# A graph-attention block with feed-forward and two normalisations: feed-forward chunks of 512 tokens in place of 256

## What is computed

```python
h = elu(gat_heads(x, adj, W_heads, a_heads))        # 4 heads, 512 features each
out = elu(gat_heads(concat(h), adj, W_out[None], a_out[None]))   # [128, 64, 512]
ffn = maximum(out @ w1 + b1, 0.0) @ w2 + b2         # 512 -> 512 -> 512
y = ffn + out
z = (y - mean(y)) / sqrt(var(y) + 1e-5) * gamma + beta
x = layernorm(x + z)                                # the output
```

## Time and profile before

| | |
|---|---|
| median of 3 runs | 2152.59 us |
| the profiled execution | 2151.31 us, span of its instructions 2149.5 us |
| TensorE busy | 2104.7 us (98% of the span) |
| VectorE, ScalarE, GpSimd busy | 1629.1 (76%), 988.9 (46%), 969.3 us (45%) |
| chain of work that ended last | TensorE 93%, VectorE 2%, GpSimd 2% |
| first feed-forward matmul | 1744.66 us from the start of the span |

### The profile page before, as it was taken

One profiled execution on the slowest core, in us unless ns is written; L12 is line 12 of the kernel. 1 busy time (PEld: TensorE's weight loads), 2 busy tenths in 40 slices (PEclk: granted clock), 3 DMA queues, 4 the chain that ended last, 5 costly groups with the idle time before them and its releaser, 6 DMA issues.

```text
span 2149.5 us, 42374 instructions
## 1 busy us (share of the span) xinstructions
PE 2104.7 (98%) x13668; PEld 1902.8 (89%) x13668; DVE 1629.1 (76%) x3297; ACT 988.9 (46%) x2282; POOL 969.3 (45%) x1017
## 2 busy tenths in 40 slices
PE   4999999999999999999999999999999999999997
PEld 2899999999999999999999999999999989999996
DVE  3877777777777777777777777777777679999998
ACT  3544444444444444444444444444444444444343
POOL 4433333333333333333333333333333347777776
PEclk7999999999999999999999999999999999999999
DMA  8111111111111111111111111111111124333342
GB/s 290 31 40 40 40 39 39 39 39 39 39 39 39 39 39 39 39 42 41 39 39 39 39 39 39 39 39 40 41 41 40 64 89 140 119 134 129 127 137 89
DMA packets 73862, 134.05 MB, mean 62 GB/s; under 512 B 8672, under 2 KB 8800, under 8 KB 73824
## 3 DMA queue, kind: packets, MB, share of 16 engines
q1 hardware_dynamic: 73824, 133.57, 18.9%
HBM read 99.98 MB, written 33.55 MB: 62 GB/s over the span
## 4 chain that ended last, share of the span: by engine, by line
PE 93%; DVE 2%; POOL 2%; issue 1%; DMA 1%; ACT 0%; SPq 0%; POOLq 0%; DVEq 0%; ACTq 0%
PE h_ps L448 11%; PE h_ps L447 11%; PE h_ps L446 11%; PE t_ps L460 11%; PE t_ps L461 11%; PE t_ps L462 11%; PE h_ps L542 3%; PE h_ps L544 3%; PE h_ps L543 3%; PE t_ps L558 2%; PE t_ps L556 2%; PE t_ps L557 2%; PE h_ps L430 1%; PE h_ps L431 1%; PE x_ps L431 1%; PE x_ps L430 1%
## 5 line engine op out<-in xcount | busy, mean ns | idle before, releaser
L1151 POOL TENSOR_TENSOR h_lo<-h_full,h_hi 128x256 fp32r<-128x256 f32 x512 | 402.8, 787 | 1012.0 <-ACT h_hi L723 998.0
L446 PE MATMUL h_ps<-g_hi,wh_hi 128*128 128x256 f32 x2048 | 585.1, 286 | 1.3 <-DVE h_full L958 0.9
L448 PE MATMUL h_ps<-g_hi,wh_lo 128*128 128x256 f32 x2048 | 578.5, 282 | 0.0
L447 PE MATMUL h_ps<-g_lo,wh_hi 128*128 128x256 f32 x2048 | 578.3, 282 | 0.0
L956 DVE TENSOR_SCALAR h_full<-h_full 128x256 f32<-128x256 f32 x512 | 247.3, 483 | 339.7 <-ACT h_full L689 338.7
L460 PE MATMUL t_ps<-wo_hi,h_hi 128*128 128x512 f32 x1024 | 404.8, 395 | 0.0
L461 PE MATMUL t_ps<-wo_lo,h_hi 128*128 128x512 f32 x1024 | 404.2, 395 | 0.0
L446 PEld LDWEIGHTS h_ps<-g_hi,wh_hi 128*128 128x128 f32 x2048 | 389.7, 190 | 16.4 <-DVE h_full L958 1.5
L447 PEld LDWEIGHTS h_ps<-g_lo,wh_hi 128*128 128x128 f32 x2048 | 390.1, 190 | 13.0
L462 PE MATMUL t_ps<-wo_hi,h_lo 128*128 128x512 f32 x1024 | 399.1, 390 | 0.0
L448 PEld LDWEIGHTS h_ps<-g_hi,wh_lo 128*128 128x128 f32 x2048 | 390.2, 191 | 0.0
(11 more groups left out here) (141 smaller groups left out, 3919.9 us busy)
## 6 DMA issues: line engine op xcount, KB each, us to landing
x_dup<-in_x SPq DMA_DIRECT2D x248, 128.0 KB, 2.5
attn<-in_x_t SPq DMA_DIRECT2D x64, 256.0 KB, 2.8
mid<-o_buf SPq DMA_DIRECT2D x64, 256.0 KB, 2.0
o_in<-mid SPq DMA_DIRECT2D x32, 512.0 KB, 3.7
x_again<-in_x SPq DMA_DIRECT2D x32, 512.0 KB, 4.3
out<-res SPq DMA_DIRECT2D x64, 256.0 KB, 2.0
wt_raw<-in_w_heads_t SPq DMA_DIRECT2D x4, 1024.0 KB, 9.3
wh_raw<-in_w_heads SPq DMA_DIRECT2D x4, 1024.0 KB, 16.4
```

The source lines that it names most:

```text
L446: mm(to, w_hi, g_hi[:, h, ft, :], start=ft == 0, stop=False)
L447: mm(to, w_hi, g_lo[:, h, ft, :], start=False, stop=False)
L448: last = mm(to, w_lo, g_hi[:, h, ft, :], start=False, stop=ft == FT - 1)
L1151: tt(h_lo[:, v % RING, :], h_full[:, v % RING, :], h_hi[:, v % RING, :].bitcast(F32), ALU.subtract)\
```

## The change

The feed-forward part goes in `FCHUNKS` = 16 chunks of `TF` = 512 tokens (`FP` = 4 pieces). The attention part is the same. In the feed-forward part:
- `hidden` uses 512 moving columns, all of a bank, and its ScalarE and GpSimd instructions are 512 wide and half as many.
- `y_ps` has four banks. The buffers of a chunk are twice as large, and some are laid over others.
- Loads are twice as large and half as many. `load_o` and `load_x_again` of chunk c + 1 now stand behind the first two stores of chunk c - 1.
- VectorE takes the norms of a chunk in two halves of two pieces. `norms(c - 1, 1)` and then `norms(c, 0)` run in the iteration of chunk c, and the four `ot_rest` of chunk c + 1 stand together between them, with the first two `y` of chunk c.
- ScalarE makes a deviation for each half: four in a chunk of 512, one of them ahead of the first hidden tile.
- Before the first chunk, four pieces are transposed in place of two, and the end of the attention part is woven into the first chunk alone.

```diff
-            hid_hi, hid_lo = sb_ff("hid_hi", [P, DT, T], F32R), sb_ff("hid_lo", [P, DT, T], F32R)
-            x_again = sb_ff("x_again", [P, 2, CP, F])
+            x_again = sb_ff("x_again", [P, 2, FP, F])
...
-        ot_ps, hid_ps, y_ps = x_ps[0], h_ps, t_ps[CHUNKS % 2]
+        ot_ps, hid_ps, y_ps = x_ps[0], h_ps, t_ps[CHUNKS % 2] + t_ps[(CHUNKS - 1) % 2]
...
             def ff_iteration(c, par, first, last):
+                if first:
+                    tail(LAST, 0)
+                    tail(LAST, 1)
+                else:
+                    save(c - 1, 0)
                 if not last and not first:
                     load_o(c + 1, 1 - par)
                     load_x_again(c + 1, 1 - par)
...
                 if not first:
-                    save(c - 1)
+                    save(c - 1, 1)
...
-                to = hid_ps[dt % 2][:, 0:T]
+                to = hid_ps[dt % 2][:, :]
...
-                zeroth, second = first_of(c), isinstance(c, int) and c == 1
-                if second:
-                    attend2(LAST, 0)
+                zeroth = first_of(c)
                 for dt in range(DT):
-                    if zeroth and dt == 3:
+                    hidden(c, dt)
+                    if zeroth and dt == 1:
                         spread2(LAST, False)
-                    if second and dt == 2:
-                        attend2(LAST, 1)
-                    hidden(c, dt)
-                for p in range(CP):
-                    if zeroth and p == 1:
-                        transpose_attn2(LAST)
+                if zeroth:
+                    transpose_attn2(LAST)
+                for p in range(FP):
                     if not last:
                         transpose_o(c + 1, 1 - par, next_turn, p)
                     result(c, p)
+                    if zeroth and p < CP:
+                        attend2(LAST, p)
...
             def ff_iteration(c, par, first, last):
-                second = isinstance(c, int) and c == 1
-                if second:
-                    out_exp(LAST, 0)
-                    t_round(LAST, LAST % 2, 1)
+                if not first:
+                    deviation(c - 1, 0, 1, mean2_done, std2_done)
                 for dt in range(DT):
...
+                    if not first and dt == 1:
+                        deviation(c - 1, 1, 0, mean_done, std_done)
...
+                    deviation(c - 1, 1, 1, mean2_done, std2_done)
+                for p in range(FP):
+                    if not last:
+                        ot_round(c + 1, p)
...
+                deviation(c, 0, 0, mean_done, std_done)
...
                 else:
-                    norms(c - 1, True, not last)
+                    sum_up(c - 1, 2)
+                    sum_up(c - 1, 3)
+                    norms(c - 1, 1)
+                for p in range(FP):
+                    if not last:
+                        ot_rest(c + 1, p)
...
+                    if p in (1, 2):
+                        sum_up(c, p - 1)
+                norms(c, 0)
```

More of the change, by code:

```diff
@@ L88, in build @@
                                            sb_ff("beta_row", [P, F]))
[L89 to L93, removed]
+            hid = sb_ff("hid", [P, 2, TF])
+            stats = sb_ff("stats", [P, 2, FP, 6])
+            moments = sb_ff("moments", [P, 2, FP, 2])
+            std = sb_ff("std", [P, 2, FP])
+            inv_std = sb_ff("inv_std", [P, 2, FP])
+            sb_ff("unused_wh", [P, 3 * F - 20 * FP])
+            o_in = sb_ff("o_in", [P, 2, FP, F])
+            hid_hi, hid_lo = sb_ff("hid_hi", [P, DT, TF], F32R), sb_ff("hid_lo", [P, DT, TF], F32R)
+            res = sb_ff("res", [P, FP, F])
         wh_lo = sb("wh_lo", [P, NH, FT, O], F32R)
@@ L115, in build @@
                 nc.sbuf_tensor("x_t_first", [P, FT, CP, P], F32R) as x_t_first:
+            pass
+        with nc.sbuf_tensor("ot_hi", [P, FT, TF], F32R) as ot_hi, \
+                nc.sbuf_tensor("ot_lo", [P, FT, TF], F32R) as ot_lo:
             pass
@@ L372, in _ @@
             load_x_again(1, 1)
[L373 to L376, removed]
+            ff_chunks(sp, ff_iteration)
+            for half in range(2):
+                save(FLAST, half)
+            for p in range(FP):
+                sp.wait_ge(store[p], 16 * FCHUNKS)
         @block.tensor
@@ L528, in transpose_o @@
                     pe.wait_ge(o_load[par], turn * 16)
-                after(pe, ot_lo_done, c * CP + p)
+                after(pe, ot_lo_done, c * FP + p)
                 for ft in range(FT):
@@ L757, in ff_iteration @@
                     if dt == 0:
-                        after(act, y_ps_done, c * CP)
+                        after(act, y_ps_done, c * FP)
                     act.activation(hid_hi[:, dt, :], hid[:, dt % 2, :], copy).then_inc(hid_hi_done, 1)
[L760 to L763, removed]
+                    if not first and dt == 1:
+                        deviation(c - 1, 1, 0, mean_done, std_done)
+                    if first and dt == 2:
+                        exps2(LAST)
                 if first:
@@ L1048, in norms, with sum_up @@
+            def sum_up(c, p):
+                dve.wait_ge(y_ps_done, c * FP + p + 1)
+                dve.wait_ge(ob_done, c * FP + p + 1)
+                tt(y[:, p, :], y_ps[p][:, :], ob[:, p, :], ALU.add).then_inc(y_done, 1)
+            def norms(c, half):
+                both = (2 * half, 2 * half + 1)
+                moments_of(c, half, 0, y, y_done, mean_done)
+                for p in both:
+                    dve.wait_ge(mean_done, c * FP + p + 1)
                     stt(z[:, p, :], y[:, p, :], moments[:, 0, p, 0:1], gamma_row[:, :], ALU.subtract,
@@ L1110, in _ @@
             dve.wait_ge(row_in, 64)
-            chunks(dve, ff_iteration)
-            norms(LAST, False, False)
+            ff_chunks(dve, ff_iteration)
+            sum_up(FLAST, 2)
+            sum_up(FLAST, 3)
+            norms(FLAST, 1)
         @block.gpsimd
```

186 lines of the change are left out of this document (89 added, 97 removed).

## The result

The changed kernel takes 2225.97 us (median of 5 runs, 2223.87 to 2229.96) against 2152.59 before: a ratio of 1.0346, 95% interval [1.0335, 1.0357]. The profiled execution took 2228.05 us, its span is 2226.3.

A forecast was written before the change was run, and what follows sets the result against it. TensorE bounds the kernel before; after, VectorE does, waiting mid-lap for TensorE. 1748.8 + 28.5 + 14 x 27.15 + 39.3 = 2196.7 us of span, plus 3.1, gives 2199.8, taken as 2200 us; range 2176 to 2233.

The forecast's parts named there:

- the ring: Loop of waits between VectorE and TensorE, one `ot_lo(0)` to the next: 27.15 us a lap, ends 25.55 to 29.35.
- A: From the end of `ot_lo(0)` to the start of `ot_lo(3)`, through TensorE's transposes and results: 7.75 us.
- E: VectorE's `norms(c, 1)`, against GpSimd's `hid_lo` and first sums: 9.3 us, between 9.16 and 9.76.
- B: VectorE's `ot_lo(3)`, from its start to the next instruction's: 0.6 us.
- D: VectorE's `y(c, 2)` and `y(c, 3)`, after the first norms: 1.2 us.
- F: VectorE's `ot_lo(0)` of the next round, closing the lap: 0.6 us.
- C: VectorE's `norms(c, 0)`, with GpSimd's sums ended before it starts: 7.7 us.
- The load: `o_in`, 1 MB, on SP's queue behind the first two stores: 5.5 us taken, hidden within 7.0 us.
- Rival 2: Load of `o_in` is the bound, from 7.0 us; at 8.5 us, 2222 us in all; chance 0.10.
- The last chunk: From TensorE's first hidden matmul of it to the last store landing: 39.3 us, nothing transposed.
- Rival 1: TensorE stays the bound, if the lap is under 23.8 us; 2148 us in all; chance 0.04.
- Rival 4: TensorE's 3.3 us of waiting per lap lowers its clock to 1.2 GHz for stretches: 2225 us; chance 0.04.

The follow-up runs named there:

- the shortest form: Changed kernel with loads ahead of stores, two banks for transposed pieces, last `ot_lo` inside `norms(c, 0)`, last `hid_lo` in two halves: 2158.43 us, 1.0034.

## Why the prediction was right, and where its sizes were off

Forecast and time lie on the same side, and the ring was there: **slower, since VectorE waits for TensorE in the middle of the lap.** By its steps:

- **A**: 7.75 us predicted, from the end of `ot_lo(0)` to the start of `ot_lo(3)`. Clean laps have 7.77 to 7.81. Six of the seven dropped laps have 9.3 to 9.4, each behind an E of 10.9: in the lap shown A is 2001.67 to 2011.02. The seventh has 10.1; there E was 9.7, but the load came so late that TensorE waited 4.0 us for it, and the clock fell behind that wait.
- **B, D, F**: 0.6 for each `ot_lo` and `y`, as shown (2011.02 to 2011.63, 2019.46 to 2020.66).
- **C**: 7.7 predicted; 7.92 in nearly every lap up to the end of `res`, 7.83 up to the start of the next instruction, which is what counts in the lap: 0.1 too little.
- **E**: this is the term that was mis-sized. 9.3 predicted; up to the end of `res` it alternates between 9.72 and 10.9, 10.3 in the mean (10.2 to the start of the next instruction). The step took the price of the norms in a chunk of the kernel before, where `hid_lo` goes in pieces of 0.96 us and other instructions meet the sums. Now its pieces take 1.42 us beside the second `z`, and the sums fall on `res`. The two runs with short instructions on GpSimd split the 2.4 us above C: 1.4 is the sums, 1.0 `hid_lo`.
- **The load**: 5.5 taken, and hidden. It takes 5.8 (the row below). The 4.4 us that the prediction worked out by the Trainium skill (DMA: Bandwidth & Descriptors, Anatomy of one DMA) were 1.4 short; the page gives that sum for transfers issued by GpSimd, and here SyncE issues them. TensorE does wait for the load, 1.9 us a lap, but VectorE is not yet free then: `ot_lo(0)` starts without a wait. Earlier loads left the clean laps at 27.74. Rival 2 is out for the changed kernel; with two banks it is what remains.
- **`hid_lo`**: 1.4 taken, mean 1.42 on the page. The start, 1748.8 predicted, was 1748.13. The first chunk took 29.84, not 28.5.
- **The last chunk**: up to the end of D it ran as summed (7.6 us after its first hidden matmul). Then E took 9.7, and `norms(15, 0)` beside GpSimd 10.9 in place of 9.6, with pairs of `z` of 2.85 and 3.24 us: 41.4 for 39.3.
- **Rival 1** (TensorE stays the bound) is out in the changed kernel, but the shortest form does it, with 23.81 us of TensorE's own work in a lap, where 23.8 was reckoned.
- **Rival 4** (the clock) had a chance of 0.04 and came true in part. Its row, the full clock in the restarts from 1740 to 1800, was weak evidence: the waits between the transposes there are 1.4 us (2.02 from one to the next, less 0.6), shorter than the 1.9 and 2.4 now. Half of the laps had 3.41 us at 1.2 GHz, at 1.6 us each in A, not the 5 of the rival's sum. That its 2225 lies 1 us from the measured time is luck: half of the surplus is E's.

The load of a chunk on the page (KB each, median us to landing), and the pairs of `z` in the last chunk:

```profile
o_in<-mid SPq DMA_DIRECT2D x16, 1024.0 KB, 5.8
```

```profile
2205.29 2.85 DVE L1067 SCALAR_TENSOR_TENSOR z<-y,moments,gamma_row 128x512 f32<-128x512 f32 x2
...
2208.25 3.24 DVE L1074 SCALAR_TENSOR_TENSOR z<-z,inv_std,xb 128x512 f32<-128x512 f32 x2
```

The sum of the span was 2196.7, and it is 2226.3. Of the 29.6 us the 14 laps hold 26.9 (406.95 against 380.1). With each step taken up to the start of the next, about 12 of them are E's, 12 are A's in the dropped laps (6 x 1.6 and 2.3), 2 are C's, and 1 is spread over the short steps. The last chunk holds 2.1, the first 1.3, and the start gives 0.7 back. So the mechanism was right, and its forecast was 26 us short by two prices in about equal parts: GpSimd's instructions beside E, and the clock, which the sum had at nothing.

## What to carry to other kernels

A wider instruction pays only where the engine that it spares is still the bound afterwards: before a change of the chunk size, write down for each bank and buffer who waits for whom in the middle of the lap, and add that ring up. Where one bank is handed to and fro between two engines, their busy shares say nothing; give it a second bank, or put other work between. And a double chunk lengthens start and end, which is paid once and here was more than all the width could gain.

## What the runs showed of the hardware

- In six laps TensorE waited 1.6 to 1.9 us for the load and 2.4 to 2.7 us for `ot_lo` one result group later, and the granted clock went to its lower level for 3.41 us each time; a seventh fall came with one wait of 4.0 us. In the clean laps, with 1.8 to 2.3 and 0.8 to 1.3 us (1.4 and 1.7 in the last), it stayed up, and so it did at a single wait of 2.85 us ahead of 1774.70. Four unread matmuls in each wait kept it up from the third chunk on. The lengths alone don't tell which lap falls: with the last `ot_lo` inside the norms, waits of 0.6 and 2.3 us went with a fall in one lap (2013.08), and 0.5 and 2.5 us with none in others.
- VectorE's `z` and `res`, which read and write SBUF, take 0.75 and 0.55 us alone, and 1.6 and 1.5 us beside GpSimd in the worst rows shown (3.24 and 2.99 for two); `ot_lo` and `y`, with an operand in PSUM, keep 0.68, and so do the statistics. In the changed kernel two `res` take 1.97 in one lap and 2.99 in the next, at almost the same place beside GpSimd's sums. Why they alternate was not found; with 256 columns in the first layer they don't.
